# Order of four scatter DMAs and a row's root on GpSimd in two attention phases of a four-layer model

## The reference

```python
x = x + tanh(g_xattn[0]) * L0_xattn(layernorm(x), ctx, ctx, mask)   # 16 heads of 16
x = x + tanh(g_ffn[0])   * L0_ffn(layernorm(x))                     # 16 experts, top 4
...
x = x + tanh(g_xattn[2]) * L2_xattn(layernorm(x), ctx)              # 16 heads of 16
x = x + tanh(g_ffn[2])   * L2_ffn(layernorm(x))                     # 16 experts, top 4, and a shared one

def L0_ffn(h):                         # L2_ffn the same with silu(x w1) w2, and a shared expert
    probs = softmax(x @ gate_w.T)
    topk_w, topk_idx = top_k(probs, 4); topk_w /= sum(topk_w)
    ...                                # for each expert e: (silu(x w1[e]) * (x w3[e])) @ w2[e]
    out = sum over the 4 experts of topk_w * expert_out
```

## Time and profile before

| | us |
|---|---|
| median of 3 runs | 1885.05 |
| lowest and highest of the 3 | 1883.65 and 1890.15 |
| the profiled execution | 1893.94 |
| its span, first to last instruction | 1892.1 |
| PE busy | 1654.8 (87%) |
| DVE, ACT, POOL busy | 1128.7, 955.8, 908.8 |
| POOL L353, sends of L0x and of L2x, 64 each | 64.9 and 64.5 busy |
| POOL L367 idle before, until DVE's mv, 48 times | 73.5 |

### The profile page before, as it was taken

The page is one execution under the profiler, slowest core; times in us unless marked ns, Lnnn a source line. Parts: engine busy times, 40 slices in busy tenths (PEclk is TensorE's granted clock), DMA queues, the critical chain, the costliest instruction groups (busy, mean ns, idle before and its releaser), DMA issues. The chain is left out here.

```text
span 1892.1 us, 37858 instructions
## 1 busy us (share of the span) xinstructions
PE 1654.8 (87%) x11810; PEld 1321.2 (70%) x11841; DVE 1128.7 (60%) x3308; ACT 955.8 (51%) x2743; POOL 908.8 (48%) x1064
## 2 busy tenths in 40 slices
PE   6999369959749999999999999879976999939997
PEld 4777258848626777777777777768855888827775
DVE  4787536628745665666666666458864353327775
ACT  3776235514414655555565555357751355517761
POOL 2366545535445554555455455134755244466620
PEclk9999679979979999999999999989997999969999
DMA  4232355545120000000000000022424244332101
GB/s 153 86 118 90 119 169 171 169 168 182 38 99 1 2 1 1 1 1 1 1 1 1 1 1 1 1 75 86 150 105 174 71 128 129 115 111 98 53 7 45
DMA packets 74546, 138.43 MB, mean 73 GB/s; under 512 B 11568, under 2 KB 56880, under 8 KB 71920
## 3 DMA queue, kind: packets, MB, share of 16 engines
q1 hardware_dynamic: 59472, 95.22, 15.8%
q0 software_dynamic: 13728, 39.60, 6.1%
q10 hardware_dynamic: 1152, 1.18, 0.2%
HBM read 85.14 MB, written 50.82 MB: 72 GB/s over the span
## 5 line engine op out<-in xcount | busy, mean ns | idle before, releaser
L1419 PE MATMUL L1f_psQ<-L1f_xT,arena 128*128 128x128 f32 x1536 | 182.0, 275 | 0.9 <-ACT L1f_xT L1495 0.9
L1419 PEld LDWEIGHTS L1f_psQ<-L1f_xT,arena 128*128 128x128 f32 x1536 | 179.1, 192 | 2.8 <-ACT L1f_xT L1495 1.1
L1290 POOL TENSOR_TENSOR L1f_rn<-L1f_ss,L1f_root_c 128x16 f32<-128x16 f32 x32 | 93.1, 2910 | 176.6 <-DVE L1f_ss L1585 176.6
L1886 POOL DMA_INDIRECT outs_L2f<-L2f_tiles_ys,L2f_tiles_spot x79 | 75.4, 955 | 130.3 <-ACT L2f_tiles_ys L2025 130.3
L1305 POOL TENSOR_TENSOR L1f_rot<-L1f_qn,L1f_sinT 128x512 f32<-128x512 f32 x64 | 111.3, 1760 | 44.9 <-DVE L1f_qn L1602 44.9
L1349 PE MATMUL L1f_psQ<-arena,L1f_hT 128*128 128x512 f32 x256 | 122.2, 622 | 0.6 <-ACT L1f_hT L1502 0.6
L1512 ACT ACTIVATE L1f_sg<-L1f_psQ,vec1f 128x128 f32<-128x128 f32 x192 | 60.0, 364 | 121.3 <-PE L1f_psQ L1419 121.1
L1631 DVE SCALAR_TENSOR_TENSOR L1f_hid<-L1f_psQ,vec1f,L1f_sg 128x128 f32<-128x128 f32 x192 | 58.6, 346 | 84.3 <-ACT L1f_sg L1512 83.0
L1295 POOL TENSOR_TENSOR L1f_pr<-L1f_pr,L1f_rs 128x512 f32<-128x512 f32 x64 | 97.4, 1542 | 22.4 <-DVE L1f_rs L1595 22.4
L1583 DVE TENSOR_REDUCE L1f_ss<-L1f_sq 128x16 f32<-128x1024 f32 x32 | 39.0, 1220 | 114.3 <-ACT L1f_sq L1476 114.3
L1886 POOL DMA_INDIRECT outs_L0f<-L0f_tiles_ys,L0f_tiles_spot x79 | 75.8, 959 | 64.8 <-ACT L0f_tiles_ys L2025 64.3
(11 more groups left out here) (487 smaller groups left out, 4625.1 us busy)
## 6 DMA issues: line engine op xcount, KB each, us to landing
L0f_tiles_xs<-rows_L0f SPq DMA_DIRECT2D x79, 144.0 KB
L2f_tiles_xs<-rows_L2f SPq DMA_DIRECT2D x79, 144.0 KB
arena<-in_w_L2f SPq DMA_DIRECT2D x8, 1120.0 KB
arena<-in_w_L1f SPq DMA_DIRECT2D x8, 1088.0 KB, 7.4
L1x_got<-outs_L0f SPq DMA_DIRECT2D x16, 512.0 KB, 3.8
L3x_got<-outs_L2f SPq DMA_DIRECT2D x16, 512.0 KB, 3.6
arena<-in_w_L0f SPq DMA_DIRECT2D x8, 768.0 KB, 4.8
rows_L2f<-zero SPq DMA_DIRECT2D x31, 144.0 KB
```

The source lines that it names most:

```text
L1290: nc.gpsimd.tensor_tensor(rn[:, s.p], ss[:, s.p], root_c[:, :], ALU.pow).then_inc(s_rn, 1)
L1419: mm = nc.tensor.matmul(out, w, xT[:, k], start=(k == 0), stop=(k == KC - 1), skip_group_check=True)
L1886: nc.gpsimd.indirect_dma_start(r.outs, bass.IndirectOffsetOnAxis(spot[:, t % YR:t % YR + 1], 0), ys[:, t % YR], None).then_inc(r.s_out[t % ...
```

## The change

One line of POOL's list in `heads_attention` changes: `sends(1)` moves from behind `roots` to in front of it. It acts in L0x and L2x, where there is a `route`; in L3x the piece of the list is empty.

```diff
@@ -546,7 +546,7 @@
                 if s.n < LATE:
                     send(nc, pool, r, s.n, range(2 * half, 2 * half + 2))
             each_round([(gather, 5), (roots, 3)] * (gathered is not None) + [(row_roots, 4)] * (gathered is None)
-                       + [(bias_row, 2), (output_bias, 2)] + [(at(sends, 0), -7), (roots, -2), (at(sends, 1), -7)] * (route is not None)
+                       + [(bias_row, 2), (output_bias, 2)] + [(at(sends, 0), -7), (at(sends, 1), -7), (roots, -2)] * (route is not None)
                        + [(keys, 2)], low_t, high_t)
```

## The result

| | before | changed |
|---|---|---|
| median of 5 runs, us | 1885.05 | 1900.43 |
| lowest, highest | 1883.65, 1890.15 | 1897.52, 1909.62 |
| profiled execution (its span) | 1893.94 (1892.1) | 1907.62 (1905.7) |

The ratio is 1.0078, with a 95% interval from 1.0057 to 1.0099. The forecast was 1886.3 us, in a range up to 1890.5.

A forecast was written before the change was run, and what follows sets the result against it. PE was taken to bound the steady rounds, and the root of sequence 15 to delay the next phase. Steady rounds 0 plus tails 2 x 0.62 gave 1.2 us: 1885.05 + 1.2 = 1886.3 us, range 1882 to 1890.5.

The forecast's parts named there:

- Price of four sends in a row: On POOL, four sends run without waiting between them take 4.95 us, read from the end of the phase.
- Steady round, cost 0: In L0x and L2x the root starts 1.2 to 1.7 us late, but ACT waits for PE's logits anyway: 0.
- The DMAs: Rows of choices 2 and 3 leave some 2.6 us earlier; only ring tile hr waits for them, eight sequences later: 0.
- What POOL gains: Steady rounds: POOL's idle 1.46 us ahead of the root is filled, keys end about 1.2 us earlier; gain 0.
- The tail: End of L0x and L2x: a send waits for DVE's row numbers, delaying root 15 and the next phase 0.62 us each.
- no cost at all: Rival: the tail's 0.62 us are hidden by a later wait before the next phase, 1885.05 us; chance 0.23.
- Slower, sends stretched beside DVE's work: Rival: moved sends stretch by 1.14 us per round beside DVE's work, passing L2x's cover, 1893 us; chance 0.06.
- The signs to look for: Timeline checks, such as sends of 0.96 to 1.1 us, ACT still waiting for logits, steady stretches unchanged within 1 us.

The follow-up runs named there:

- e10: The changed kernel, unchanged, run on chip 12 (second kind): 1868.58 us, 0.9969 of the kernel before.
- e9: The kernel before, unchanged, run again for a profile on chip 12 (second kind): 1874.75 us, ratio 0.9999.
- e14: The changed kernel with a 0.97 us memset behind its four sends, ahead of the root, on chip 13: 1894.17 us, 1.0044 of the kernel before.
- e4: The changed kernel with one memset between its two pairs of sends, on chip 1: 1882.62 us, 0.9981 of the kernel before.
- e17: The changed kernel with the memset between its two pairs of sends, on chip 15: 1887.83 us, 0.9970 of the kernel before.
- e1: The changed kernel with the root first, then the four sends in a row, on chip 1: 1913.29 us, 1.0135 of the kernel before.
- e15: The changed kernel with sent rows of 128 bytes in L2x and L2f, features left out, on chip 13: ratio 1.0074 to the kernel before.
- e16: The kernel before with memsets between the pairs of the 16 sends of L2f, on chip 15: 1888.14 us against 1892.73, ratio 0.9967.
- e18: The changed kernel, unchanged, run once more on chip 15: 1908.55 us, 1.0074 of the kernel before.

## Why the prediction was wrong, step by step

- *Price of four sends in a row*, 4.95 us: right to the hundredth (153.33 to 158.28).
- *Steady round, cost 0* (1.4 us of cover in L0x, 0.58 in the tightest round of L2x): right as far as it went. On the second kind of chip the rounds are unchanged, and on the first ACT's wait ahead of the logits is still there (0.98 to 2.76 us in 131 to 189 us). But the step priced the moved sends as POOL's time alone.
- *The DMAs*, "0": **this is the step that failed.** It asked who waits for the sends and found only the ring tile. It did not ask whom a longer train disturbs. On the chip of the comparison that is worth 8.9 us in L0x and 7.1 in L2x (the price of 0 for this term, and 16.0 measured). Four in a row stood in the kernel before too, at 186.71, with two idle times of 1.8 us marked "remote" beside them, and 16 in a row with one of 13.17 us. These rows were not read. The views that would have shown them were ACT's and DVE's waits by releaser: the prediction took PE's alone, and PE itself hardly waits in the steady rounds.
- *What POOL gains*, 0 in the rounds: right.
- *The tail*, 2 x 0.62 us: its first half was right. DVE's end came 0.80 us later (e10 against e9), held by the row numbers of the batch of 10 and 11, as forecast; the send starts 0.29 us behind them, not 0.1, which makes the 0.62 into 0.80. Its second half was wrong. The 3.3 us in the earlier trace rows were read as following DVE, but they follow POOL's last send by 5.28 us, and the phase came 1.40 us *earlier*. The rival "no cost at all" had pointed at just this gap.
- *Slower, sends stretched beside DVE's work* (0.06, 1893): not what happened. The moved sends took 0.96 to 1.08 us. The sign was right, the mechanism another. The Trainium skill, page "SBUF — State Buffer", section "Who interferes with whom", which was weighed there, also says that PE and ACT wait for nobody at SBUF's ports. It speaks of ports only, and the 1.6 us that DVE waits here for finished matmuls are no case of it that the traces could show.
- *The signs to look for* worked. "If the length of the steady stretches changes by more than 1 us" was named as what would prove the forecast wrong.

What is shown: the loss goes with the whole train and not with the root's lateness (e14 against e4 and e17, e1, e10), nor with the bytes (e15), and it exists in the comparison and on the chips 1, 13 and 15, not on 12 and 14. What stays open: by what way a train of POOL's DMAs reaches PE's results, and what the two kinds are. Each chip was used for one group only, so "kind of chip" may as well be something that differed between the hours of the groups. Pairs hold results back on the first kind as well (7 in the kernel before, by up to 0.54 us, and 0 in e9), and the rounds of the kernel before are 0.4 to 0.6 us longer there (11.13 to 11.26 against 10.60 to 10.77), but a kernel without any pair was not tried.

Of the gain of 5.8 us on chip 12, the two phase ends explain 2.8. The two profiles show no gain at all: e9 took 1868.49 us and e10 1869.07, since e10 gets back 2.8 us at the phase ends and lies 2.9 us behind by the longer start. But e9's profile is of the fastest of its ten executions. Over all of them the kernel before had a median granted clock of 0.950 on this chip and the changed one 0.953, so that the rest goes together with the clock. Whether the change does that stays open.

On the first kind the changed order with a pause (e4 0.9981, e17 0.9970) and the paced L2f (e16 0.9967) were fastest; the first of them did not run on the second kind. Pacing the 16 sends of L2f costs nothing on the second kind (1.0002, 0.9998) and gained in its one run on the first (0.9967), so of the edits tried on both it is the only one that lost nowhere.

## What to carry to other kernels

Before bundling DMAs on one queue, look at what stands beside the bundles that the kernel already has: read the idle times of *every* engine there, and take one that is marked "remote", or put down to an engine that had long been done, as a question and not as noise. To find what releases a phase, compare the distances to each engine's last work in two places: the one that stays the same (here 5.28 us behind POOL) is the one that counts. And a change whose sign depends on the chip is only known once it has run on more than one.

## What the runs showed of the hardware

- The same kernel took 1885 to 1893 us in the comparison and on the chips 1, 13 and 15, and 1870 to 1876 on 12 and 14. The median of the mean granted clocks of its executions was 0.948, 0.947 and 0.9465 on the chips 1, 13 and 15, 0.950 on 12 and 0.953 on 14. The clock isn't all of it: in the rounds 8 to 12 of L0x it reads 1.00 in the comparison and in e9 alike, and they last 11.13 to 11.26 and 10.60 to 10.77 us. On the first kind PE's results come late beside trains of POOL's indirect DMAs, in the changed kernel 0.62 to 1.16 us behind a send's end.
- More work on an engine can be cheaper than less: a memset of 0.97 us between two pairs of sends, 24 times, made the kernel 1.0% faster than without (0.9970 against 1.0074 on chip 15).
- The first 30 us come in two lengths, whatever the kernel: the first scores of L0x stand at 27.2 to 27.9 us or at 30.4 to 30.6. In the later case PE's matmul groups of L594 take 2.04 us for the second sequence as they do for the first in both, instead of 1.13, and the granted clock reads 1.00 in both. The changed kernel has shown both (30.40 in the comparison and in e10, 27.27 in e18), so the 3 us are no part of the change.
